# Routing weights of a two-expert mixture made on ScalarE and placed by GpSimd, instead of on VectorE

## The reference, cut to what matters

```python
scores = xf @ Wr + br                                  # 8 scores a token
_, top_idx = jax.lax.top_k(scores, 2)
mask = jax.nn.one_hot(top_idx, 8).sum(-2) > 0
router_weights = jax.nn.softmax(jnp.where(mask, scores, -jnp.inf), axis=-1)
h = jax.nn.gelu(jnp.einsum('td,edp->etp', xf, W1) + b1[:, None, :])
y = jnp.einsum('etp,epd->etd', h, W2) + b2[:, None, :]
out = jnp.einsum('te,etd->td', router_weights, y)
```

## Time and profile before

| | |
|---|---|
| median of 3 runs | 1010.74 us (1009.75 to 1011.5) |
| the profiled execution's own time | 1011.38 us |
| its span, first to last instruction | 1009.6 us |
| busy: PE, DVE, ACT, POOL | 902.7, 733.6, 479.1, 427.0 us |
| mean granted TensorE clock | 0.968 of full speed |
| attention stage | about the first 500 us |
| expert stage | about the last 500 us |

### The profile page before, as it was taken

How to read it: one execution, slowest core, us unless ns; L and a number is a source line. 1 busy time by engine, 2 the same in 40 slices (tenths; PEclk the granted TensorE clock), 3 DMA queues, 4 the chain that set the end, 5 groups by cost and what they waited for, 6 DMA issues and landing times.

```text
span 1009.6 us, 27138 instructions
## 1 busy us (share of the span) xinstructions
PE 902.7 (89%) x7313; PEld 743.9 (74%) x7314; DVE 733.6 (73%) x1909; ACT 479.1 (47%) x1548; POOL 427.0 (42%) x452
## 2 busy tenths in 40 slices
PE   4989999999999999997189999999999989999895
PEld 4556655656655656654179998999999989999895
DVE  2469999999999999997646666666566666666663
ACT  1556566666566665563034434343434433434432
POOL 5335665555655555653213333333323323233233
PEclk9789999999999999998579999999999999999998
DMA  7901111111111111111282222222222222222221
GB/s 240 375 27 52 54 45 51 53 39 52 53 42 53 53 38 53 53 38 39 83 278 40 39 37 37 38 43 32 43 32 43 39 36 38 37 38 38 39 39 24
DMA packets 51451, 62.68 MB, mean 62 GB/s; under 512 B 6273, under 2 KB 46930, under 8 KB 51282
## 3 DMA queue, kind: packets, MB, share of 16 engines
q1 hardware_dynamic: 38546, 44.36, 13.9%
q0 software_dynamic: 12864, 17.83, 10.3%
HBM read 38.91 MB, written 23.27 MB: 62 GB/s over the span
## 4 chain that ended last, share of the span: by engine, by line
PE 61%; DVE 14%; issue 9%; DVEq 6%; ACT 3%; SPq 3%; DMA 3%; POOL 0%; ACTq 0%; POOLq 0%
PE p_a L1084 19%; PE p_cum L1084 8%; PE p_z L1084 8%; PE p_qk L1084 8%; PE p_vg L1084 7%; PE p_o L1084 6%; DVE w_hi L842 4%; SPq L444 2%; PE p_tr L1084 1%; PE p_tr L1266 1%; DMA host_x<-in_L_attn_x_dram 1%; DVE x L917 1%; PE p_o L1103 1%; DVE host_s_r L1068 1%; DVEq L1033 1%
## 5 line engine op out<-in xcount | busy, mean ns | idle before, releaser
L641 POOL DMA_INDIRECT out_dram<-x,tok x68 | 163.6, 2405 | 344.3 <-DVE x L1061 318.7
L661 ACT ACTIVATE h2T<-p_tr,mods 128x128 f32<-128x128 f32 x200 | 80.6, 453 | 345.0 <-PE p_tr L1266 290.3
L1084 PE MATMUL p_a<-w_hi_r,host_s_r 128*128 x544 | 145.2, 299 | 11.8 <-DVE host_s_r L1068 11.8
L1084 PE MATMUL p_a<-w_r,host_s_r 128*128 x544 | 139.8, 289 | 0.0
L590 POOL TENSOR_TENSOR w<-qkT_both,own_half 128x512 f32<-128x512 f32 x64 | 65.0, 1035 | 165.4 <-ACT qkT_both L735 155.8
L1038 DVE COPY host_x<-w 128x1024 f32 x68 | 47.3, 696 | 98.0 <-issue 52.0
L1084 PEld LDWEIGHTS p_a<-w_hi_r,host_s_r 128*128 128x128 f32 x544 | 101.8, 187 | 14.2 <-issue 13.9
L1084 PEld LDWEIGHTS p_a<-w_r,host_s_r 128*128 128x128 f32 x544 | 101.9, 187 | 0.3
L842 DVE TENSOR_TENSOR w_hi<-p_a,upto 128x512 f32<-128x512 f32 x128 | 84.3, 679 | 4.1 <-PE p_a L1084 4.1
L621 POOL DMA_INDIRECT expert_rows<-rows,pos x64 | 63.9, 999 | 51.7 <-POOL rows L618 22.5
L1084 PE MATMUL p_qk<-h2T,host_x 128*128 128x128 f32 x544 | 68.8, 281 | 7.0 <-DVE qkT_both L1038 5.9
(11 more groups left out here) (208 smaller groups left out, 2085.4 us busy)
## 6 DMA issues: line engine op xcount, KB each, us to landing
w<-in_L_ffn_W_dram SPq DMA_DIRECT2D x16, 1024.0 KB, 12.5
ln_host<-expert_rows SPq DMA_DIRECT2D x68, 136.0 KB, 2.1
host_x<-in_L_attn_x_dram SPq DMA_DIRECT2D x64, 128.0 KB, 2.1
out_dram<-x SPq DMA_DIRECT2D x32, 128.0 KB, 1.7
w<-in_L_wmod_dram SPq DMA_DIRECT2D x1, 1536.0 KB, 6.4
expert_rows<-pad_rows SPq DMA_DIRECT2D x8, 136.0 KB, 1.8
out_dram<-x,tok POOLq DMA_INDIRECT x68, 4.7
b_all<-in_L_ffn_b_dram SPq DMA_DIRECT2D x1, 1024.0 KB, 7.5
```

The lines of the kernel that those rows point to most:

```text
L641: nc.gpsimd.indirect_dma_start(out=out, out_offset=bass.IndirectOffsetOnAxis(ap=tok[u][:, 0:1], axis=0), in_=y_out[u][:], in_offset=None, ...
L661: last = A.activation(dst[:, j, :], src[:, j * P:(j + 1) * P], ACT.Identity, scale=mods[:, which + 2 + j:which + 3 + j], bias=mods[:, whic ...
L1084: return nc.tensor.matmul(dst, lhsT, rhs, start=start, stop=stop, skip_group_check=True)
```

## The change

ScalarE makes both weights as exponentials. With l = ln(1+exp(g)) the weights are exp(-l) and exp(g-l). Its four operations (exp, ln, exp, exp) stand behind the 1/sqrt of x1's statistics and in front of the three exponentials that end in `e_ready`; the one exp(g) that stood between L725 and L731 is gone from there. VectorE's L927, L928, L934, L935 and L936 are gone. GpSimd multiplies the two one-hot rows by the weights (128 x 2 x 8) and adds the two products into the row (128 x 8), between its copy of the token's number and its scatters. VectorE has two new waits, in front of the gap (L887) and in front of `hot[0]` (L889), since the buffers are now read by other engines.

```diff
@@ VectorE, route part
                     ro.then(V.max_index(top_i[:], top[:], score[:]))
+                    after(dve, weights_ready, r)
                     V.tensor_tensor(gap[:], top[:, 1:2], top[:, 0:1], ALU.subtract).then_inc(gap_ready, 1)
                     ro.then(V.tensor_copy(top_f[:], top_i[:, 0:TOP]))
+                    after(dve, gates_placed, r)
-                    ro.mark(V.tensor_scalar(hot[0][:], iota_e[:], top_f[:, 0:1], None, ALU.is_equal))
+                    ro.mark(V.tensor_scalar(hot[0], iota_e[:], top_f[:, 0:1], None, ALU.is_equal))
...
                     yo.mark(V.bn_stats(st_1[:], x1[v][:]))
-                if route:
-                    dve.wait_ge(gap_exp, r + 1)
-                    ro.then(V.tensor_scalar(wt[:, 0:1], gap_e[:], 1.0, None, ALU.add))
-                    ro.mark(V.reciprocal(wt[:, 1:2], wt[:, 0:1]))
-                if finish:
                     yo.sync(apart=True)
                     V.bn_aggr(mv_1[:, 0:2], st_1[:]).then_inc(x1_stats, 1)
-                if route:
-                    ro.sync()
-                    ro.mark(V.tensor_tensor(wt[:, 2:3], gap_e[:], wt[:, 1:2], ALU.mult))
-                    ro.then(V.tensor_scalar(wt_a[:], hot[0][:], wt[:, 1:2], None, ALU.mult))
-                    V.scalar_tensor_tensor(out=rows[u][:, D:D + E], in0=hot[1][:], scalar=wt[:, 2:3],
-                                           in1=wt_a[:], op0=ALU.mult, op1=ALU.add)
@@ ScalarE
-                if route:
-                    act_e.wait_ge(gap_ready, s - 1)
-                    A.activation(gap_e[:], gap[:], ACT.Exp).then_inc(gap_exp, 1)
...
                 if finish:
                     inverse_root(mv_1, s - 1, x1_stats, x1_scale)
+                if route:
+                    act_e.wait_ge(gap_ready, s - 1)
+                    weight.begin(s - 2)
+                    weight.then(A.activation(gap_e[:], gap[:], ACT.Exp))
+                    after(act_e, gates_placed, s - 2)
+                    weight.then(A.activation(gap_l[:], gap_e[:], ACT.Ln, bias=1.0))
+                    A.activation(wt[:, 0:1], gap_l[:], ACT.Exp, scale=-1.0)
+                    A.activation(wt[:, 1:2], gap_l[:], ACT.Exp, scale=-1.0, bias=gap[:, 0:1]).then_inc(weights_ready, 1)
                 if front:
                     act_e.wait_ge(cum_ready, f + 1)
@@ GpSimd, route part
                     nc.gpsimd.tensor_copy(rows[u][:, ID:ID + 1], ids[:, bass.ds(r, 1)]).then_inc(id_ready, 1)
-                    wait_apart(pool, (id_ready, r + 1), (pos_ready, r + 1))
+                    pool.wait_ge(chosen_ready, r + 1)
+                    pool.wait_ge(weights_ready, r + 1)
+                    nc.gpsimd.tensor_tensor(wt_hot[:], hots[:], wt[:].unsqueeze(2).to_broadcast([P, TOP, E]),
+                                            ALU.mult).then_inc(wt_hot_ready, 1)
+                    pool.wait_ge(wt_hot_ready, r + 1)
+                    nc.gpsimd.tensor_tensor(rows[u][:, D:D + E], wt_hot[:, 0], wt_hot[:, 1],
+                                            ALU.add).then_inc(gates_placed, 1)
+                    wait_apart(pool, (id_ready, r + 1), (gates_placed, r + 1), (pos_ready, r + 1))
```

More of the change, by code:

```diff
@@ L207, in build @@
         top_f = sb("top_f", [P, TOP])
-        hot = [sb(f"hot{j}", [P, E]) for j in range(TOP)]
+        hots = sb("hots", [P, TOP, E])
+        hot = [hots[:, j] for j in range(TOP)]
         chosen = sb("chosen", [P, E], BF16)
@@ L211, in build @@
         gap_e = sb("gap_e", [P, 1])
-        wt = sb("wt", [P, 3])
-        wt_a = sb("wt_a", [P, E])
+        gap_l = sb("gap_l", [P, 1])
+        wt = sb("wt", [P, TOP])
+        wt_hot = sb("wt_hot", [P, TOP, E])
         base = sb("base", [P, E])
@@ L332, in build @@
         gap_ready = sem("gap_ready")
-        gap_exp = sem("gap_exp")
+        weights_ready = sem("weights_ready")
+        wt_hot_ready = sem("wt_hot_ready")
+        gates_placed = sem("gates_placed")
+        act_w = sem("act_w")
         chosen_ready = sem("chosen_ready")
@@ L656, in _ @@
             A.activation(cnd_e[:], cnd[:], ACT.Exp, scale=-1.0).then_inc(cond_exp, 1)
-            order, gate = Order(act_e, act_f), Order(act_e, act_g)
+            order, gate, weight = Order(act_e, act_f), Order(act_e, act_g), Order(act_e, act_w)
             def modulate(dst, src, which, sm):
@@ L886, in step @@
                     ro.then(V.max_index(top_i[:], top[:], score[:]))
+                    after(dve, weights_ready, r)
                     V.tensor_tensor(gap[:], top[:, 1:2], top[:, 0:1], ALU.subtract).then_inc(gap_ready, 1)
                     ro.then(V.tensor_copy(top_f[:], top_i[:, 0:TOP]))
[L889 to L891 removed]
+                    after(dve, gates_placed, r)
+                    ro.mark(V.tensor_scalar(hot[0], iota_e[:], top_f[:, 0:1], None, ALU.is_equal))
+                    ro.then(V.tensor_scalar(hot[1], iota_e[:], top_f[:, 1:2], None, ALU.is_equal))
+                    V.tensor_tensor(chosen[:], hot[0], hot[1], ALU.add).then_inc(chosen_ready, 1)
                 if front:
@@ L961, in step @@
                     ro.sync()
-                    ro.mark(V.tensor_tensor(pick[0][:], hot[0][:], slot[:], ALU.mult))
-                    ro.then(V.tensor_tensor(pick[1][:], hot[1][:], slot[:], ALU.mult))
+                    ro.mark(V.tensor_tensor(pick[0][:], hot[0], slot[:], ALU.mult))
+                    ro.then(V.tensor_tensor(pick[1][:], hot[1], slot[:], ALU.mult))
                     ro.mark(V.tensor_reduce(pos_f[:, 0:1], pick[0][:], AX_X, ALU.add))
```

## The result

| | before | after |
|---|---|---|
| median | 1011.50 us (11 runs, 1008.92 to 1013.46) | 1013.82 us (11 runs, 1012.99 to 1016.38) |
| profiled execution, span | 1009.6 us | 1014.0 us |
| DVE, ACT, POOL busy | 733.6, 479.1, 427.0 us | 673.0, 495.4, 444.4 us |
| a step of the loop, mean of 25 | 13.80 us | 13.94 us |
| from x1 to the product that waits for `e_ready` | 3.41 us | 3.52 us |

The ratio is 1.0031 with a 95% interval of 1.0021 to 1.0040, so the change costs 2.1 to 4.0 us, 3.1 in the middle. The direction is the one forecast; the size, +8.5 us, was more than twice too large. VectorE lost 60 us of busy time and the kernel became slower.

What follows compares the result with a forecast made beforehand. The prediction took a ring of waits through VectorE, PE and ScalarE to bound each step, no engine being full. ScalarE's slot (4.4 us) plus VectorE's waits (4.1) gave +8.5 us, so 1019 us, range 1010.5 to 1026.

Steps and rivals of the forecast that it cites:

- Removing the five operations: VectorE between x1 and L942: covered by PE's and ScalarE's arc, so 0 us a step.
- The slot on ScalarE: Four small operations in front of L744's exponential: it starts 0.15 us later a step, 4.4 us over 29 steps.
- The two waits on VectorE: New waits at L887 and L889: 0.07 us each, 0.14 us a step, 4.1 us over 29 steps.
- GpSimd's products: Two small products behind GpSimd's copy, 0.6 to 1.0 us in front of the scatters: hidden, 0 us.
- Rival C: GpSimd's products block VectorE's hT_lo (L848), up to 0.27 us each time, 7.8 us on top, 1027 us; chance 0.12.
- Last steps: Steps 31 to 33: five operations partly in the open against two waits, opposite signs, both under 1 us together: 0.
- Rival B: exp(g) gone from ScalarE lets GpSimd's L590 start earlier and VectorE gain: 3.2 us less, 1007.5 us; chance 0.12.
- the rule on the shared port: VectorE instructions with two SBUF inputs and GpSimd ones reading SBUF lock each other out; alone it suggested 64 us gained.

Runs made afterwards that it cites:

- b_nofive: The kernel before without VectorE's five small operations and nothing in their place: 1010.37 us, ratio 0.9986 to 1.0004.
- b_waits: The kernel before with two more long-met waits on VectorE, in front of the gap and hot[0]: 1010.30 us, ratio 0.9986 to 1.0006.
- a_late: The changed kernel with ScalarE's four small operations moved behind its last copy of the step: 1011.75 us, ratio to before 0.9992 to 1.0010.
- late_lo: a_late with GpSimd's two products given a wait for VectorE's hT_lo that was already met: 1010.17 us, ratio to before 0.9984 to 1.0004.
- a_plus3: The changed kernel with three more independent small exponentials on ScalarE, between exp(-l) and exp(g-l): 1021.27 us, ratio to before 1.0082 to 1.0120.
- late_ranks: a_late with TensorE's ranks moved right behind its wait for x1 and VectorE's positions in front of L950: 1004.29 us, ratio to before 0.9928 to 0.9961.

## Why the prediction was wrong

- *Removing the five operations is worth nothing: right.* 3.40 against 3.41 us in step 1 foretold b_nofive.
- *The slot on ScalarE: right in place and size.* L762 starts 0.86 us behind the exponential, as summed; x1 to L762 is 2.58 us in place of 2.43, the 0.15 forecast; the spacing that I had taken as 0.20 is 0.18, that behind ln 0.24 in place of 0.22, and the extra wait in front of ln costs nothing (0.22 with it, as summed without). 0.03 to 0.04 came back behind it: the three exponentials follow each other a little closer (from L744's start to the end of L748 0.93 us, from L762's to L766's end 0.91), and L950 starts 0.03 us behind the last of them, where L942 started 0.05 behind, as b_nofive's arc of 3.39 has it too. 29 x 0.12 = 3.5 us; forecast 4.4.
- *The two waits on VectorE: the step that failed, a cost put on something that has none here.* "The second wait costs 0.09; ... I take 0.07. L887 and L889 get one each: 0.14 us a step", 4.1 us of the 8.5. Measured: 0.00 in the trace after and in b_waits. I had read the distance of L872 from its source as the price of its second wait. L872 is another instruction behind another kind of source, and the row doesn't say what its 0.12 us are; that stays open. What it isn't is a price of any second wait. The lower bound, 0, was in the text; I took a value near the other end on one row.
- *GpSimd's products: hidden, but for 0.03 us in eleven steps,* 0.3 us. Rival C had the mechanism and a price nine times too high, because I took the block by a product of 256 columns for one of 16.
- *Last steps: 0.35 us less,* forecast 0.
- With 0 for the waits the sum is 4.4 us, 1015.1 us; the measured 1013.8 lies 1.3 us below that and 5.2 below the 1019 that I gave, though inside the range.
- Rival B (faster, by GpSimd starting earlier) did not occur: GpSimd's L595 does start earlier, 0.04 us ahead of x1 where L590 started 0.05 behind it, but its decays wait for `e_ready` (0.20 us idle in front of L607). Nor did it in a_late, where `e_ready` is not later.
- Of the rule on the shared port (the Trainium skill, "SBUF — State Buffer", Who interferes with whom): by it the five operations looked like 64 us; they were long, blocked, and their time was worth nothing until something else was put in its place. That it was GpSimd that made them long shows behind the last x1 of the trace before: there GpSimd does nothing from 482.04 to 488.36, and L934, L935 and L936, from 485.59 on, take 0.16, 0.22 and 0.23 us in place of 0.74, 0.77 and 0.65. The trace agrees with the rule at L934, which has two SBUF inputs, and at `hT_lo` (L868) in late_lo. L935 has one tensor and a scalar for each partition, so it is not the case that the rule as I gave it speaks of; the trace shows it blocked all the same.

## What to carry to other kernels

Where two engines run side by side between a release and a join, take the work off the one that arrives last; time freed on the other is worth nothing by itself. It becomes worth something when work from behind the join is moved into it: here, with the four small operations also put behind the release, a loss of 3 us turned into a gain of 4 to 7, and into one of 14 to 17 with an exchange in TensorE's list on top, which was tried only with that move. And small operations put "into an idle slot" of an engine have to be summed with their dependent spacings (0.22 to 0.24 us here for one that waits for the last, 0.09 to 0.11 for one that doesn't, 0.18 behind one with a pointer operand) against the slot's length before its next release.

## What the runs showed that I had not expected

- A long-met wait on VectorE in front of an operation that already waits for its predecessor costs nothing measurable (0.03 us from end to start at the gap with one wait and with two; b_waits, 13.70 / 13.89 us a step as before).
- ScalarE's small independent exponentials cost 0.09 us each in a row of four (a_plus3), less than the 0.11 between two of different kinds.
- A scatter that GpSimd issues and VectorE's normalisation of x can be in each other's way. In late_ranks the scatter ran from 301.96 to 303.11 and L810, which starts at 302.65, took 0.55 us; 0.54 to 0.56 is what it takes in nearly every step of the loop, always with the scatter still running. In the kernel after, where it starts behind the scatter, it takes 0.41 in all 32. Early in late_ranks L810 once takes 0.41 with the scatter running as well, so the overlap alone does not settle it, and the cause is not shown (timeline, late_ranks):

```profile
301.96 1.15 POOL L633 DMA_INDIRECT expert_rows<-rows,pos  x1 [0.30 <-issue]
302.65 0.55 DVE L810 TENSOR_SCALAR host_n<-host_x,mv_x 128x256 f32<-128x256 f32 x1 [0.31 <-ACT mv_x L684]
```
